# Moving the base inverse's steps and the state update's work between VectorE, ScalarE and PSUM in a delta-rule attention kernel

## The chip, the cores and the metric

The kernel runs on 1 core of a Trainium2 chip, as one program. The metric is the time of an execution in device microseconds. PE is TensorE (PEld its weight loads), DVE is VectorE, ACT is ScalarE, POOL is GpSimd, and SP is SyncE, which issues most DMAs.

## The reference

The input x is [2, 1024, 512] in float32. Four blocks are added to it in turn: a gated delta-rule attention (A), a feed-forward block with 4-bit weights, a state-space scan, and the feed-forward block again. The change touches only A. Cut to what matters, A computes, for each batch and each of 32 value heads (two share one key head; keys and values have 128 channels):

```python
q, k, v = split(silu(causal_conv4(x @ w_qkv)))      # 16, 16 and 32 heads of 128
beta, g = sigmoid(x @ w_b), -exp(A_log) * softplus(x @ w_a + dt_bias)
q, k = l2norm(q) / sqrt(128), l2norm(k)
def step(state, q_t, k_t, v_t, g_t, b_t):           # for each of the 1024 tokens
    state = state * exp(g_t)
    delta = (v_t - k_t @ state) * b_t
    state = state + outer(k_t, delta)
    return state, q_t @ state
core = norm_w * rmsnorm(outs) * silu(x @ w_z)
x = x + core @ w_out
```

## The kernel before

**Units and slots.** The work of the attention is cut into 32 units: a unit is one batch and one key head with its two value heads (REP = 2). The 1024 tokens are 8 chunks of 128 (NC = 8). Every engine runs a loop over slots, 8 slots per unit, and in each slot does pieces of several units at different stages: `unit_at_only(slot, offset)` gives the unit n with slot = 8 n + offset. The order of instructions in each engine's queue is written out by hand, and engines wait for each other by semaphores (`wait_ge`, `then_inc`). In the text, **place k** is a slot whose number modulo 8 is k. A unit starts its projections at offset 0, the convolution's taps at offsets 2, 4, 6 and 8, its decay weights at 8 to 11, the Gram products at 8 to 13, the inverse at 10 to 19, the scan over its chunks at offset 16 + t (t = 0 to 7, so chunk t of some unit is at place t), and the output product at 23 + t.

**The scan of one chunk, t > 0, in a slot.** PE multiplies K with the state (L712, into bank KB), then Q with the state (L717) and transposes K (L719), both into QB. DVE makes the residual from K's product (L1333). PE runs product "a" and perhaps "b" of a later unit's projection (L676), turns a finished o (L761), and multiplies the triangular inverse with the residual (L780), into bank UB. ACT copies that to `u` (L1046). After product "c", PE multiplies the scaled K with u (L810, the addition to the state, into KB) and the decay-weighted Q K product with u (L814, into UB). ACT scales Q's product by exp(gc) into `q_state` (L958) and K by a weight into `k_scaled` (L967). DVE updates the state from KB (L1406; a copy L1399 for t = 0) and adds `q_state` to UB's product into `o` (L1417; a copy L1414 for t = 0). ACT squares o for the norm (L1127). Then PE does the output product (L831), which needs DVE's gated `oT` (L1291), made from L761.

**The base inverse.** Each unit has two halves (a = 0, 1) of four chunks. The inverse of the 16 x 16 blocks is done on DVE by `base_inverse`: section 0 (L1167 to L1178) turns and masks the blocks, and then 14 steps j = 1 to 14, each a shuffle (L1186), a product (L1188) and a sum (L1190) whose width is 8 j; last the identity is added (L1194). Before the change, half 0 does section 0 at offset 10 behind the gate and half 1 at the end of offset 14; steps 1 to 6 (section 1) come at offset 11 + 4a behind the taps, steps 7 to 10 (section 2) at the end of that slot, steps 11 to 14 with the identity (section 3) at the end of offset 12 + 4a. POOL masks the result into `inv` (L1519), DVE turns it (L1198) and PE widens it to 128 x 128 in three levels (L605 to L627), for which ACT makes negated copies `off` (L1068, L1074, L1075, L1081, L1082) and copies back (L1108 to L1116). L608 waits for L1068, and L617 for the last L1075.

**Other work on the path.** The projection's products are read out by ACT (`read_product`, L910 to L917) and, two of seven, by DVE (L1277). ACT starts the convolution with the last tap (L1008), waiting for the reads of both; DVE adds three taps (L1306): two in the middle of the slot, one after the o addition. ACT's SiLU is at places 5 and 1 with two table loads around it. `decay` gets a subtraction on DVE (L1371), a select on POOL (L1505) and an exponential on ACT (L1092), for half 0 at offset 8 and for half 1 at offsets 9, 9 and 11. L910 to L917, L1008 and the u copy L1046 stand in one queue: ACT takes them in the order in which the slot lists them.

Of the kernel before, what the change touches and what calls it, by code (L numbers as in the profile page):

```python
# [13 lines left out]
P = 128  # L14
# [179 lines left out]
def unit_at_only(slot, offset):  # L194
# [10 lines left out]
    rows_turned xn_turned gate_sum gc_sum gc_turned product sums ss_turned g_pair v_turned inv_pe ks qs_kt u_pe s_pe a_pe  # L205
    oT_pe wout_pe
    taps rate ln_a xnT softplus_a e_gc gc_rows act_read tap3 silu ss_copy ln norm_exp chunk_exp decay_exp v_evict q_state
    k_scaled u_copy squares z_silu rstd_ln rstd inv_act
    stats xn gate_in softplus g_in gc gates dve_read conv col_beta decay_sub lT a_weight base inv_dve resid state o_add
# [5 lines left out]
def attention(nc, ctx, c, banks, dram, x_in, x_out, early):  # L215
    on = signals(nc, ctx, ATTENTION_SIGNALS)
    with ExitStack() as st:
# [38 lines left out]
        state, resid, u, q_state = (sb(name, [P, REP, P]) for name in ("state", "resid", "u", "q_state"))  # L256
# [258 lines left out]
        def tensor(e):  # L515
# [184 lines left out]
            for slot in range(ATTENTION_SLOTS):  # L700
# [63 lines left out]
                if n_scan is not None:  # L764
# [11 lines left out]
                    if at > 0:  # L776
                        e.wait_ge(on["o_add"], at)
                    for r in range(REP):
                        rhs = resid[:, r, :] if t > 0 else v_tok[:, N % 2, 0, r, :]
                        made = e.matmul(two(UB, 0)[:, r, :], invT[:, t, r, :], rhs, start=True, stop=True)  # L780
# [19 lines left out]
                if n_scan is not None:  # L800
# [5 lines left out]
                    if t % HALF == 0:  # L806
                        e.wait_ge(on["a_weight"], 4 * N + 2 * (t // HALF) + 2)
                    if t < NC - 1:
                        for r in range(REP):
                            made = e.matmul(two(KB, REP * P)[:, r, :], k_scaled[:, r, :], u[:, r, :],  # L810
                                            start=True, stop=True)
                        made.then_inc(on["s_pe"], 1)
                    for r in range(REP):
                        made = e.matmul(two(UB, REP * P)[:, r, :], decay[:, s, r, t, :], u[:, r, :],  # L814
                                        start=True, stop=True)
# [33 lines left out]
        def scalar(e):  # L849
# [92 lines left out]
            for slot in range(ATTENTION_SLOTS):  # L942
# [8 lines left out]
                if n_scan is not None:  # L951
# [3 lines left out]
                    if t > 0:  # L955
                        e.wait_ge(on["o_add"], at)
                        for r in range(REP):
                            made = e.activation(q_state[:, r, :], two(QB, 0)[:, r, :], ACT.Copy,  # L958
                                                scale=e_gc[:, N // HK, REP * (N % HK) + r, t:t + 1])
                        made.then_inc(on["q_state"], 1)  # L960
# [4 lines left out]
                    if t < NC - 1:  # L965
# [3 lines left out]
                        made.then_inc(on["k_scaled"], 1)  # L969

# [9 lines left out]
                for a in range(2):  # L980
                    n = unit_at_only(slot, 5 + 4 * a)
                    if n is not None:
                        N = n
                        e.wait_ge(on[f"decay{a}{N % 2}"], 16 * (N // 2 + 1))
                        if n >= 2:
                            e.wait_ge(on["state"], LINKS * (N - 2) + 4 * a + 4 - a)
# [1467 lines left out]
```

## Time and profile before

| | us |
|---|---|
| median of 3 runs (lowest to highest) | 4167.84 (4165.18 to 4172.16) |
| the profiled execution | 4168.05 |
| its span, first to last instruction | 4166.1 |
| PE busy | 3997.3 (96%) |
| DVE busy | 3196.9 (77%) |
| ACT busy | 2592.6 (62%) |
| POOL busy | 958.8 (23%) |

The attention takes about the first 3000 us of the span; the mean granted clock of TensorE was 0.991 of its full speed. Busy time is a share of the whole span, so an engine at 77% can still be full for whole slots. In the timeline a row has start, duration, engine, line, operation, out<-in, shapes and count; "[0.45 <-DVE resid L1333]" says that the engine stood idle for 0.45 us before it and what ended that. Consecutive instructions of one line are merged, and the next instruction of a queue may start shortly before the last one's end. The rows of one unit are shown, from about 1800 to 1888 us.

### The profile page before, as it was taken

What the parts mean: (1) busy time and instruction counts of PE and PEld (TensorE: products, weight loads), DVE (VectorE), ACT (ScalarE), POOL (GpSimd) and SP (SyncE); (2) the same over time, 40 slices, a digit from 0 to 9 for tenths busy, and PEclk for the clock granted to TensorE, in tenths of its full rate; (3) what the DMA queues carried; (4) which work ended last, traced back from release to release, by engine and by line L of the source; (5) the groups of instructions that cost most, each with busy time, mean ns of one, the idle gap of its engine ahead of it and who ended that gap; (6) DMA issues with size and microseconds to landing.
All of it is one profiled execution on the core that took longest, in us unless ns stands there. A gap on an engine that the chain in (4) does not pass through costs nothing. (4 is left out here: it accounts for less than half of the span.)

```text
span 4166.1 us, 83038 instructions
## 1 busy us (share of the span) xinstructions
PE 3997.3 (96%) x29437; PEld 2282.0 (55%) x29437; DVE 3196.9 (77%) x8334; ACT 2592.6 (62%) x6087; POOL 958.8 (23%) x1110
## 2 busy tenths in 40 slices
PE   7999999999999999999999999998899999999999
PEld 4555556556555555566565555555444444444444
DVE  4777887787787777877778877777447989898940
ACT  3566676666666666666666666666445656574643
POOL 1224333234333243333333333332100000000000
PEclk9999999999999999999999999999999999999999
DMA  3223334333433433343334333334304545454510
GB/s 131 83 72 84 87 86 90 85 80 85 92 77 85 120 82 85 90 86 85 81 87 92 75 87 85 82 80 97 83 1 132 164 148 168 147 175 153 183 57 10
DMA packets 290733, 402.99 MB, mean 97 GB/s; under 512 B 25774, under 2 KB 125362, under 8 KB 290258
## 3 DMA queue, kind: packets, MB, share of 16 engines
q1 hardware_dynamic: 253458, 330.57, 26.1%
q0 software_dynamic: 36864, 67.13, 12.0%
q8 instruction: 236, 3.87, 0.4%
q14 instruction: 175, 1.43, 0.1%
HBM read 288.56 MB, written 113.25 MB: 96 GB/s over the span
## 5 line engine op out<-in xcount | busy, mean ns | idle before, releaser
L676 PE MATMUL bank<-x_blocks,rows_b 128*128 128x512 f32 x1536 | 713.0, 597 | 0.9 <-ACT partial L914 0.9
L1306 DVE SCALAR_TENSOR_TENSOR conv<-raw,conv_w,conv 128x1024 f32<-128x1024 f32 x384 | 522.7, 1361 | 61.9 <-ACT conv L1008 56.8
L676 PE MATMUL bank<-x_blocks,w_pair 128*128 128x512 f32 x1152 | 549.9, 605 | 14.8 <-DVE x_blocks L1277 4.5
L831 PE MATMUL bank<-w_out_unit,oT 128*128 128x512 f32 x1008 | 491.4, 610 | 0.9 <-ACT out_stage L931 0.9
L676 PEld LDWEIGHTS bank<-x_blocks,rows_b 128*128 128x128 f32 x1536 | 274.9, 190 | 249.1 <-issue 231.3
L1662 PE MATMUL bank<-xnT_f,w_gu 128*128 128x512 f32 x704 | 324.5, 605 | 1.2 <-ACT xnT_f L2161 0.9
L1291 DVE SCALAR_TENSOR_TENSOR oT<-bank,norm_w,z 128x256 f32<-128x256 f32 x252 | 119.2, 473 | 261.4 <-PE bank L761 260.3
L676 PEld LDWEIGHTS bank<-x_blocks,w_pair 128*128 128x128 f32 x1152 | 206.8, 193 | 205.5 <-issue 169.5
L2231 ACT ACTIVATE step_decay<-dt,rate 128x512 f32<-128x512 f32 x256 | 183.4, 720 | 217.1 <-DVE h L2340 215.0
L1681 PE MATMUL bank<-w_down,hidden 128*128 128x512 f32 x704 | 316.9, 594 | 1.7 <-DVE x_blocks L1740 1.7
L1671 PE MATMUL bank<-xnT_f,w_gu 128*128 128x512 f32 x704 | 316.8, 593 | 0.5 <-DVE hidden L1702 0.5
L1127 ACT ACTIVATE k_scaled<-o 128x128 f32<-128x128 f32 x512 | 154.0, 302 | 227.5 <-DVE o L1417 175.4
L1469 POOL DMA_DIRECT2D x_after<-out_stage x256 | 223.0, 904 | 149.8 <-ACT out_stage L931 144.6
L831 PEld LDWEIGHTS bank<-w_out_unit,oT 128*128 128x128 f32 x1008 | 173.1, 192 | 128.0 <-issue 121.9
L1519 POOL TENSOR_TENSOR inv<-n_base,slot_mask 128x512 f32<-128x512 f32 x64 | 81.5, 1274 | 647.7 <-DVE n_base L1194 647.7
L1188 DVE TENSOR_TENSOR rows_b<-rows_b 128x8 f32<-128x8 f32 (+13 forms) x896 | 200.2, 223 | 30.8
L1190 DVE TENSOR_TENSOR n_base<-n_base,rows_b 128x8 f32<-128x8 f32 (+13 forms) x896 | 199.7, 223 | 30.8
L931 ACT COPY out_stage<-bank 128x512 f32<-128x512 f32 x256 | 148.4, 580 | 108.4 <-PE bank L831 99.9
L1681 PEld LDWEIGHTS bank<-w_down,hidden 128*128 128x128 f32 x704 | 130.4, 191 | 152.0 <-issue 151.9
L1662 PEld LDWEIGHTS bank<-xnT_f,w_gu 128*128 128x128 f32 x704 | 132.7, 195 | 147.2 <-issue 145.7
L1671 PEld LDWEIGHTS bank<-xnT_f,w_gu 128*128 128x128 f32 x704 | 130.8, 191 | 149.9 <-issue 148.2
L1186 DVE STREAM_SHUFFLE rows_b<-n_base 128x8 f32<-128x8 f32 (+13 forms) x896 | 207.2, 231 | 0.0
(270 smaller groups left out, 8360.8 us busy)
## 6 DMA issues: line engine op xcount, KB each, us to landing
x_after<-out_stage POOLq DMA_DIRECT2D x256, 256.0 KB, 4.2
rows_b<-bc_rows SPq DMA_DIRECT2D x256, 256.0 KB, 3.6
rows_c<-bc_rows SPq DMA_DIRECT2D x256, 256.0 KB, 3.7
w_pair<-in_w_qkv SPq DMA_DIRECT2D x128, 256.0 KB, 3.9
decay<-gc_rows SPq DMA_DIRECT2D x64, 512.0 KB, 5.0
z<-z_rows SPq DMA_DIRECT2D x64, 512.0 KB, 5.1
z_rows<-x_blocks SPq DMA_DIRECT2D x96, 256.0 KB, 5.8
w_pair<-in_w_z SPq DMA_DIRECT2D x64, 256.0 KB, 3.3
```

Source lines behind the costliest of these rows:

```text
L676: made = e.matmul(bank[:, :], weight[:, j, :], part(0, m)[:, j, :], start=j == 0 and m in (1, 5), stop=j == 1, skip_group_check=True)
L831: made = e.matmul(out_rows(N, t)[:, :], turned_to(N, t)[:, r, :], w_out[:, N % 2, r, :], start=r == 0, stop=r == REP - 1)
L1127: made = e.activation(squares[:, r, :], o[:, at % O_RING, r, :], ACT.Square, accum_out=o_rstd[:, N % 2, t, r:r + 1])
L1186: e.stream_shuffle(row, cols, lanes).then_inc(on["base"], 1)
L1188: e.tensor_tensor(row, row, col, ALU.mult).then_inc(on["base"], 1)
L1190: e.tensor_tensor(cols, cols, row, ALU.add).then_inc(on["base"], 1)
L1306: e.scalar_tensor_tensor(acc, raw[:, i, tap:tap + T], conv_w[:, tap, col:col + 1], acc, ALU.mult, ALU.add).then_inc(on["conv"], 1)
L1469: e.dma_start(x_out[n // HK][t * P:(t + 1) * P, :], out_stage[:, at % STAGES, :], accum_op=ALU.add).then_inc(on[f"x_added{at % STAGES}"], 16)
L1662: made = e.matmul(GB[:, :], w_gu[:, j, i * P:(i + 1) * P], xnT[:, R % 2, j, :], start=j == 0, stop=j == KT - 1)
L1671: made = e.matmul(UB[:, :], w_gu[:, j, INNER + i * P:INNER + (i + 1) * P], xnT[:, R % 2, j, :], start=j == 0, stop=j == KT - 1)
L1681: made = e.matmul(DB[t][:, :], hidden[:, U % 2, t * P:(t + 1) * P], w_down[:, i, :], start=i == 0, stop=i == IT - 1)
L2231: e.activation(step_decay[:, (p + 2) % DECAY_RING, :], dt[:, (KT * q + i) % 2, :], ACT.Exp, scale=rate[:, i, n:n + 1]).then_inc(on["step_d ...
```

## The change

Three things are changed. (1) The base inverse has five sections in place of four, with other slots and earlier points in them: section 0 at offset 10 + 4a, steps 1 to 3 at 11 + 4a and steps 11 to 14 at 12 + 4a all stand ahead of the "a" read and the gate; steps 4 to 10 stand behind the middle taps and ahead of the "b" read. The subtraction and the select for half 1 go from offset 9 to 10. (2) The state's sum and o's sum are formed in PSUM: ACT writes Q's scaled product and (t = 1 to 6) the scaled old state into bank UB, and L810 and L814 add to them there (start=False). DVE then only copies the state out, once both are done. (3) ACT copies o out of UB in place of DVE's addition. The product of L780 goes to bank KB. In front of its seeds ACT now makes `k_scaled`.

```diff
             e.wait_ge(on["inv_dve"], INV_STEPS * (2 * N + t // HALF + 1))
-        if at > 0:
-            e.wait_ge(on["o_add"], at)
         for r in range(REP):
             rhs = resid[:, r, :] if t > 0 else v_tok[:, N % 2, 0, r, :]
-            made = e.matmul(two(UB, 0)[:, r, :], invT[:, t, r, :], rhs, start=True, stop=True)
+            made = e.matmul(two(KB, REP * P)[:, r, :], invT[:, t, r, :], rhs, start=True, stop=True)
         made.then_inc(on["u_pe"], 1)
...
             e.wait_ge(on["a_weight"], 4 * N + 2 * (t // HALF) + 2)
+        if t > 0:
+            e.wait_ge(on["seeded"], LINKS * N + t)
+        elif at > 0:
+            e.wait_ge(on["o_copy"], at)
         if t < NC - 1:
             for r in range(REP):
-                made = e.matmul(two(KB, REP * P)[:, r, :], k_scaled[:, r, :], u[:, r, :],
-                                start=True, stop=True)
-            made.then_inc(on["s_pe"], 1)
+                made = e.matmul(two(UB, 0)[:, r, :], k_scaled[:, r, :], u[:, r, :],
+                                start=t == 0 and r == 0, stop=True, skip_group_check=True)
         for r in range(REP):
             made = e.matmul(two(UB, REP * P)[:, r, :], decay[:, s, r, t, :], u[:, r, :],
-                            start=True, stop=True)
+                            start=False, stop=True, skip_group_check=True)
         made.then_inc(on["a_pe"], 1)
...
         e.wait_ge(on["qs_kt"], at + 1)
-        if t > 0:
-            e.wait_ge(on["o_add"], at)
-            for r in range(REP):
-                made = e.activation(q_state[:, r, :], two(QB, 0)[:, r, :], ACT.Copy,
-                                    scale=e_gc[:, N // HK, REP * (N % HK) + r, t:t + 1])
-            made.then_inc(on["q_state"], 1)
         if t % HALF == 0:
...
             made.then_inc(on["k_scaled"], 1)
+        if t > 0:
+            e.wait_ge(on["o_copy"], at)
+            for r in range(REP):
+                made = e.activation(two(UB, REP * P)[:, r, :], two(QB, 0)[:, r, :], ACT.Copy,
+                                    scale=e_gc[:, N // HK, REP * (N % HK) + r, t:t + 1])
+            if 0 < t < NC - 1:
+                e.wait_ge(on["state"], LINKS * N + t)
+                e.wait_ge(on["chunk_exp"], 2 * N + t // HALF + 1)
+                for r in range(REP):
+                    made = e.activation(two(UB, 0)[:, r, :], state[:, r, :], ACT.Copy,
+                                        scale=chunk_decay[:, N % 2, r, t:t + 1])
+            made.then_inc(on["seeded"], 1)
...
             if n >= 2:
-                e.wait_ge(on["state"], LINKS * (N - 2) + 4 * a + 4 - a)
+                e.wait_ge(on["seeded"], LINKS * (N - 2) + 4 * a + 4 - a)
             e.activation(chunk_decay[:, N % 2, :, HALF * a:HALF * (a + 1)],
...
         e.wait_ge(on["u_pe"], 8 * (n_scan) + t_scan + 1)
-        e.mul(u[:, :, :], two(UB, 0), 1.0 if t_scan == 0 else -1.0).then_inc(on["u_copy"], 1)
+        e.mul(u[:, :, :], two(KB, REP * P), 1.0 if t_scan == 0 else -1.0).then_inc(on["u_copy"], 1)
...
         at = 8 * N + t
-        e.wait_ge(on["o_add"], at + 1)
+        e.wait_ge(on["a_pe"], at + 1)
+        if t < NC - 1:
+            e.wait_ge(on["state"], LINKS * N + t + 1)
+        if at >= O_RING:
+            e.wait_ge(on["oT_pe"], at - O_RING + 1)
+        e.copy(o[:, at % O_RING, :, :], two(UB, REP * P)).then_inc(on["o_copy"], 1)
+        e.wait_ge(on["o_copy"], at + 1)
         if at > 0:
...
     for j in range(1, BASE - 1):
-        if section == (1 if j < 7 else 2 if j < 11 else 3):
+        if section == (1 if j < 4 else 2 if j < 7 else 3 if j < 11 else 4):
             lanes = [16 * (lane // 16) + j for lane in range(32)]
...
         done += 3
-    if section == 3:
+    if section == 4:
         e.wait_ge(on["base"], done)
...
     for a in range(2):
-        n = unit_at_only(slot, 8 + a)
+        n = unit_at_only(slot, 8 + 2 * a)
         if n is not None:
...
             turn_base()
+    for a in range(2):
+        for section, at in ((0, 10), (1, 11), (4, 12)):
+            n = unit_at_only(slot, at + 4 * a)
+            if n is not None:
+                base_inverse(n, a, section)
     read_at(slot, "a")
     gate_out(slot)
-    n = unit_at_only(slot, 10)
-    if n is not None:
-        base_inverse(n, 0, 0)
     convolve(slot, (2, 1))
         if n is not None:
-            base_inverse(n, a, 1)
+            base_inverse(n, a, 2)
+            base_inverse(n, a, 3)
...
         at = 8 * N + t
-        if t == 0:
-            e.wait_ge(on["s_pe"], LINKS * N + 1)
-            e.tensor_copy(state[:, :, :], two(KB, REP * P)).then_inc(on["state"], 1)
-        elif t < NC - 1:
-            e.wait_ge(on["s_pe"], LINKS * N + t + 1)
-            if t in (1, HALF):
-                e.wait_ge(on["chunk_exp"], 2 * N + t // HALF + 1)
-            e.wait_ge(on["state"], LINKS * N + t)
-            for r in range(REP):
-                made = e.scalar_tensor_tensor(
-                    state[:, r, :], state[:, r, :], chunk_decay[:, N % 2, r, t:t + 1],
-                    two(KB, REP * P)[:, r, :], ALU.mult, ALU.add)
-            made.then_inc(on["state"], 1)
-        e.wait_ge(on["a_pe"], at + 1)
-        if at >= O_RING:
-            e.wait_ge(on["oT_pe"], at - O_RING + 1)
-        if t == 0:
-            e.tensor_copy(o[:, at % O_RING, :, :], two(UB, REP * P)).then_inc(on["o_add"], 1)
-        else:
-            e.wait_ge(on["q_state"], LINKS * N + t)
-            e.tensor_tensor(o[:, at % O_RING, :, :], two(UB, REP * P), q_state[:, :, :], ALU.add).then_inc(
-                on["o_add"], 1)
+        if t < NC - 1:
+            e.wait_ge(on["a_pe"], at + 1)
+            e.tensor_copy(state[:, :, :], two(UB, 0)).then_inc(on["state"], 1)
...
             turn_inverse(a)
-        n = unit_at_only(slot, 10 + 4 * a)
-        if n is not None and a == 1:
-            base_inverse(n, a, 0)
-        n = unit_at_only(slot, 11 + 4 * a)
-        if n is not None:
-            base_inverse(n, a, 2)
-        n = unit_at_only(slot, 12 + 4 * a)
-        if n is not None:
-            base_inverse(n, a, 3)
+
         def gpsimd(e):
...
     for a in range(2):
-        n = unit_at_only(slot, 8 + a)
+        n = unit_at_only(slot, 8 + 2 * a)
         if n is not None:
             e.wait_ge(on["decay_sub"], 2 * N + a + 1)
```

## Rows read from the trace of the kernel before

**Rows 1.** The page, part 1: busy time of each engine.

```profile
PE 3997.3 (96%) x29437; PEld 2282.0 (55%) x29437; DVE 3196.9 (77%) x8334; ACT 2592.6 (62%) x6087; POOL 958.8 (23%) x1110
```

**Rows 2.** The waits of PE: engine line, waited for, us, times, longest.

```profile
PE bank L780 <- DVE resid L1333: 52.5, 64, 4.2
```

**Rows 3.** Timeline of PE, places 5 and 1: start, us, what, idle before.

```profile
1815.54 0.71 PE L780 MATMUL bank<-resid,invT 128*128 128x128 f32 x4 [0.45 <-DVE resid L1333]
...
1858.60 0.71 PE L780 MATMUL bank<-resid,invT 128*128 128x128 f32 x4 [1.02 <-DVE resid L1333]
```

**Rows 4.** Groups by line, whole span: busy us, mean ns, idle before.

```profile
L1406 DVE SCALAR_TENSOR_TENSOR state<-state,chunk_decay,bank 128x128 f32<-128x128 f32 x384 | 115.6, 343 | 46.6 <-PE bank L810 38.6 <-issue 0.2
...
L1417 DVE TENSOR_TENSOR o<-bank,q_state 128x256 f32<-128x256 f32 x224 | 93.4, 417 | 2.0 <-PE bank L814 2.0
...
L1371 DVE TENSOR_TENSOR decay<-decay,col_beta 128x1024 f32<-128x1024 f32 x64 | 78.1, 1220 | 3.7 <-DVE col_beta L1365 0.5
...
L958 ACT ACTIVATE q_state<-bank,e_gc 128x128 f32<-128x128 f32 x448 | 140.0, 365 | 79.1 <-PE bank L719 57.7 <-PE bank L717 21.4
```

**Rows 5.** Timeline of DVE, place 7 to place 1.

```profile
1838.62 0.48 DVE L1291 SCALAR_TENSOR_TENSOR oT<-bank,norm_w,z 128x256 f32<-128x256 f32 x1 [1.24 <-PE bank L761]
...
1840.98 0.18 DVE L1186 STREAM_SHUFFLE rows_b<-n_base 128x32 f32<-128x32 f32 x1
...
1848.94 3.36 DVE L1306 SCALAR_TENSOR_TENSOR conv<-raw,conv_w,conv 128x1024 f32<-128x1024 f32 x2
...
1852.22 0.41 DVE L1399 COPY state<-bank 128x256 f32<-128x256 f32 x1
...
1854.09 0.25 DVE L1186 STREAM_SHUFFLE rows_b<-n_base 128x88 f32<-128x88 f32 x1
...
1857.94 0.60 DVE L1333 SCALAR_TENSOR_TENSOR resid<-bank,e_gc,v_tok 128x128 f32<-128x128 f32 x2
```

**Rows 6.** Timeline of POOL, place 0.

```profile
1848.78 1.09 POOL L1505 TENSOR_SCALAR_AFFINE_SELECT decay<-decay 128x1024 f32<-128x1024 f32 x1 [2.78 <-DVE decay L1371]
```

**Rows 7.** Timeline of PE, place 1.

```profile
1852.69 0.70 PE L712 MATMUL bank<-state,kq 128*128 128x256 f32 x2
...
1863.80 0.75 PE L608 MATMUL bank<-off,inv_turned 32*32 32x32 f32 x64
```

**Rows 8.** Timeline of ACT, place 1.

```profile
1853.00 0.31 ACT L1127 ACTIVATE k_scaled<-o 128x128 f32<-128x128 f32 x1 [1.61 <-DVE o L1414]
...
1855.68 0.58 ACT L914 COPY partial<-bank 128x512 f32<-128x512 f32 x1 [0.48 <-PE bank L676]
...
1862.71 0.47 ACT L1068 ACTIVATE off<-bank,neg_odd 128x256 f32<-128x256 f32 x1
```

**Rows 9.** Timeline of DVE, place 2.

```profile
1866.94 0.61 DVE L1333 SCALAR_TENSOR_TENSOR resid<-bank,e_gc,v_tok 128x128 f32<-128x128 f32 x2
...
1869.20 0.69 DVE L1277 TENSOR_TENSOR raw<-bank,partial 128x512 f32<-128x512 f32 x1 [1.65 <-PE bank L676]
...
1871.54 1.83 DVE L1167 STREAM_TRANSPOSE l_quads<-lT 32x256 f32<-32x256 f32 x4
...
1874.46 2.60 DVE L1306 SCALAR_TENSOR_TENSOR conv<-raw,conv_w,conv 128x1024 f32<-128x1024 f32 x2
```

**Rows 10.** Timeline of ACT, and of PE in the last row, place 2.

```profile
1869.92 1.15 ACT L1008 ACTIVATE conv<-raw,conv_w 128x1024 f32<-128x1024 f32 x1 [1.31 <-DVE raw L1277]
...
1874.02 0.27 ACT L1075 ACTIVATE off<-bank 32x128 f32<-32x128 f32 x1
...
1875.10 0.22 PE L617 MATMUL bank<-invT,off 32*32 32x32 f32 x2
```

**Rows 11.** Timeline of ACT, and of PE in the last row, place 5.

```profile
1813.19 0.58 ACT L917 COPY raw<-bank 128x512 f32<-128x512 f32 x1 [0.58 <-PE bank L676]
...
1820.26 0.47 ACT L1068 ACTIVATE off<-bank,neg_odd 128x256 f32<-128x256 f32 x1
...
1820.87 0.74 PE L608 MATMUL bank<-off,inv_turned 32*32 32x32 f32 x64
```

More of the change, by code:

```diff
@@ L204 @@
     z_store0 z_store1 z_store2 z_load0 z_load1
-    rows_turned xn_turned gate_sum gc_sum gc_turned product sums ss_turned g_pair v_turned inv_pe ks qs_kt u_pe s_pe a_pe
+    rows_turned xn_turned gate_sum gc_sum gc_turned product sums ss_turned g_pair v_turned inv_pe ks qs_kt u_pe a_pe
     oT_pe wout_pe
-    taps rate ln_a xnT softplus_a e_gc gc_rows act_read tap3 silu ss_copy ln norm_exp chunk_exp decay_exp v_evict q_state
+    taps rate ln_a xnT softplus_a e_gc gc_rows act_read tap3 silu ss_copy ln norm_exp chunk_exp decay_exp v_evict seeded o_copy
     k_scaled u_copy squares z_silu rstd_ln rstd inv_act
-    stats xn gate_in softplus g_in gc gates dve_read conv col_beta decay_sub lT a_weight base inv_dve resid state o_add
+    stats xn gate_in softplus g_in gc gates dve_read conv col_beta decay_sub lT a_weight base inv_dve resid state
     part_sum oT_copy out_copy
@@ L255, in attention @@
         oT = sb("oT", [P, REP, P])
-        state, resid, u, q_state = (sb(name, [P, REP, P]) for name in ("state", "resid", "u", "q_state"))
+        state, resid, u = (sb(name, [P, REP, P]) for name in ("state", "resid", "u"))
         k_scaled = sb("k_scaled", [P, REP, P])
```

## The prediction, made before the change was run

> **What bounds the kernel now.** I read the page first. PE is busy for 3997 of 4166 us [rows 1], so nothing that leaves PE's own work alone can win more than the 169 us in which it idles. The change leaves it alone: every matmul stays, with the same shapes. So the question is what PE waits for. The waits of PE have one entry that stands out: L780, the product of the inverse with the residual, waits 52.5 us in 64 pieces for L1333, the residual that DVE makes [rows 2]. 64 is two per unit, and the timeline shows them: 0.45 us at place 5 and 1.02 us at place 1 [rows 3]. A place is the slot number modulo 8, so each comes once per unit. All 32 units look alike (32 x 1.47 = 47 us), so one unit worked out at its places gives the whole.
>
> DVE is late there because of the base inverse: at the end of places 4 and 0 it runs the last steps, widths 88 to 112, and only then the residual. At place 0 that is from 1854.09 to 1857.94, and the residual comes right behind [rows 5]. The change takes this chain out of the residual's way. Whether it wins depends on what those steps are put in front of instead.
>
> **Work that moves between engines.** DVE loses L1406 (115.6 us) and L1417 (93.4 us) [rows 4] and gets a copy of 0.41 us per slot [rows 5], 192 of them (places 1 to 6) beyond the 32 that it makes now: 209 - 79, or 130 us less in all, about 4 us per unit. ACT gets the o copy (256 slots; I take 0.37 us from L958's mean) and a second pair of scaled copies at places 1 to 6, at 0.6 us a pair (L958: 140.0 us for 224 pairs [rows 4]): 95 + 115 = 210 us. ACT is at 2593 us [rows 1], so it has room on the average. These totals cost PE nothing by themselves; what counts is where each engine has no idle time before something that PE needs. The new wait of L810 for the seeds costs nothing: ACT queues them before the u copy, which L810 waits for anyway. What it may cost is 0.6 us on the u copy; cover is PE's own product c, which runs between L780 and L810. The copy to state now waits for the second pair of matmuls (L814) too, some 0.5 us, covered by the output product that PE runs before it needs the state. The decay subtraction of half 1 goes from place 1 to place 2. No DMA is moved; SP keeps its waits. On POOL the mask comes earlier and the select of half 1 one slot later, both with slack.
>
> **Place 0 to 1: the state is late.** From the gate at 1838.62 (place 7, started by PE) DVE has no idle time until the state copy at 1852.22 [rows 5]: 13.60 us of queue. PE starts the next slot at 1852.69, 0.06 us after that copy ends [rows 7]. So the margin is nil, and what is added to this stretch is paid. What goes: the first three steps of the inverse (1839.03 to 1840.98, 1.95 us), which now run before the gate in idle time, and an o addition (0.42, [rows 4]). What comes: the last four steps with the identity (1854.09 to 1857.94, 3.85 us), now ahead of gate, taps and state. 13.60 - 1.95 - 0.42 + 3.85 = 15.08: the state is 1.48 us later, and PE with it. The stall of 1.02 us at L780 is then gone (only one tap, half of 2.60 us [rows 9], is queued between the state and the residual), which leaves 0.46.
>
> The same slot's end on ACT: its squares started at 1853.00, behind the o of DVE [rows 8]. Now the state copy ends at 1854.11, the o copy takes 0.37 and the squares start near 1854.55, 1.55 later. ACT then has one idle piece of 0.48 us before L914 [rows 8], against 0.6 us of new seeds: 1.55 + 0.12 = 1.67 us late when it comes, behind two table loads and the silus, to L1068, which starts now at 1862.71 and takes 0.47. That gives 1864.85, and PE takes 0.14 us to follow it (1820.73 to 1820.87 [rows 11]): L608 at 1864.99 where it was 1863.80 [rows 7]. **Cost: 1.2 us**, in 31 units (the last has no next unit beside it).
>
> **Place 2: the first tap is late.** Here the base inverse's section 0 and the moved subtraction are put ahead of the product read L1277. Section 0 takes 1871.54 to 1874.46, 2.92 us [rows 9], the subtraction 1.22 [rows 4]. DVE idles 1.65 us before that read now [rows 9], so the read is 4.14 - 1.65 = 2.5 us later. ACT's tap L1008 waits for exactly this read [rows 10] and stands before the u copy and the copies L1074 and L1075 in its queue. The last of these ends at 1874.29 now and PE wants it at 1875.10 [rows 10]. Later by 2.5 it ends at 1876.8, and L617 starts at 1876.9, 1.8 us late. ACT has small waits in between that shrink; I take **1.5 us**, in the 30 units in which section 0 and the tap fall together. Bounds: 0, if the work were hidden, and 2.5.
>
> **Place 5: the win is given back.** L780's 0.45 us goes here, since place 4 has room: the steps go where DVE now waits for the gate's transpose. But L608 follows ACT's L1068 by only 0.14 us (1820.26 + 0.47 against 1820.87 [rows 11]): ACT sets that moment, from a product read at 1813.19 which itself waits for PE and has 0.58 us of idle before it [rows 11], about the seeds' 0.6. So ACT is no earlier and PE waits there instead. Gain 0, bounds 0 and 0.45.
>
> **Sum**, against the profiled execution's own 4168.05 us: 31 x 1.2 + 30 x 1.5 = 37 + 45 = 82 us, so 4250. The median of the runs is 4167.84, the same.
>
> **Two prices not seen in the trace.** (a) No ACT copy from SBUF into PSUM. Nearest is L958, from PSUM: 0.6 us a pair; between 0.4 and 0.75 a place-1 chain moves by 0.2. (b) DVE beside POOL. The two taps at place 0 take 3.36 us with POOL's select beside them and 2.60 at place 2 [rows 5, 6, 9]: 0.76 us lost. The 3.28 us to the state copy in my sum hold that loss once. After the change the select falls beside the moved steps, and POOL's mask, which follows the moved steps, can fall beside the taps. Between no loss (the state 0.76 earlier) and a second one (0.76 later) I keep one.
>
> **Rivals.**
> A, faster, 0.16: the spread works as written. For it: the 52.5 us [rows 2] are real and DVE has 130 us less to do. If every stall at L780 goes and nothing takes its place, 4168 - 52 = 4116. With ACT setting L608 at places 1 and 5, the win is the slack at place 1 only (L608 at 1863.80, ACT ready at 1862.71 + 0.47 + 0.14 = 1863.32: 0.48 us): 4168 - 15 = 4153. It decides at the state copy of place 0: if DVE reaches it no later than 0.5 us after now, no loss. Against: the margin of 0.06 [rows 5, 7].
> B, only place 0 costs, 0.18: the read at place 2 is late but ACT catches up before L617. 4168 + 37 = 4205.
> C, POOL's mask beside DVE, 0.12: what the select did to the taps [rows 5, 6] happens twice at place 0. 31 x 0.76 = 24 more: 4274. The Trainium skill, SBUF — State Buffer (Who interferes with whom), has a rule: a DVE operation with two SBUF inputs and a GpSimd operation that reads SBUF exclude each other for the whole instruction. By that rule, the trace agrees for the select beside the taps, if not for its full 1.09 us [rows 6]; and by it a mask over the taps would cost as C says.
> D, ACT becomes the bound, 0.08: 0.6 us of seeds reach PE at all of the 192 slots: 4168 + 115 = 4283. Against: at place 4 and 6 ACT idles beside product reads now.
> E, even, 0.06: the losses equal the 15 to 30 us won.
> The forecast, both places costing as worked out, 0.40; its own range is 4215 to 4285.
>
> **Numbers.** Faster: A, 0.16; within 0.2% (8 us, about what the measurement can tell from no change): E, 0.06; slower: the rest, 0.78. The range runs from 4140 (the upper part of A) to 4285 (C, the bounds of place 2), leaving out the clean win and the worst of C and D.
>
> **What would show it.** L780's wait for L1333 near 0 in every case. If I am right: PE's L712 waits for the state L1399's successor about 1.5 us once per unit; L617 waits for L1075 about 1.5 us once per unit; L608 waits for L1068 by 0.7 us at place 1 and 0.5 at place 5; ACT's L1008 waits for L1277 near 4 us at place 2; the unit is 2.5 us longer. If L617 does not wait, the step at place 2 is wrong; if L712 does not, the one at place 0; if PE's waits in the scan are all below 0.1 us, A holds. PE's busy time should stay at 3997 us: if it grows, the accumulating matmuls cost more than the plain ones, which I excluded.

## The result, and the profile after the change

The changed kernel takes **4362.99 us** (median of 5 runs, 4356.47 to 4363.45), where the kernel before took 4165.18 us beside it (4162.54 to 4172.16): a ratio of **1.0466**, 95% interval 1.0450 to 1.0481. It is 198 us slower. The forecast was 82 us slower, 4250, with a range up to 4285: the sign was right, the size was not.

First the page of the changed kernel, its span and part 1, against [rows 1]:

```profile
span 4360.9 us, 83006 instructions
...
PE 4026.4 (92%) x29437; PEld 2284.0 (52%) x29437; DVE 3238.2 (74%) x7886; ACT 2771.1 (64%) x6727; POOL 1029.3 (24%) x1110
```

PE issues the same 29437 matmuls. DVE is busy 41 us longer, though it lost the sums for the state and o. The first two experiments (e1, e2) separate this: with the PSUM part alone DVE is busy 3083.9 us, 113 less than before (the forecast had 130), and with the spread alone 3354.4 us, 157.5 more, with the same 8334 instructions as before. So with the spread the same instructions take longer; the rows below show some of them beside POOL. ACT and POOL are busy longer too. Next the waits of PE (engine, what line waited for what, us in total, times, longest). The one entry of [rows 2], L780's wait for the residual, is no longer among the large ones. In its place stand nine others ("..." stands for a single wait at the start):

```profile
PE bank L608 <- ACT off L1075: 43.7, 62, 1.7
PE bank L676 <- DVE raw L1290: 43.7, 33, 2.6
PE bank L617 <- ACT off L1082: 34.2, 31, 1.1
PE bank L832 <- DVE oT L1304: 30.0, 32, 1.3
PE bank L712 <- DVE state L1415: 27.4, 31, 1.6
PE bank L574 <- ACT v_tok L877: 19.6, 31, 2.1
PE bank L676 <- ACT bank L911: 17.8, 35, 1.5
PE bank L812 <- ACT u L1053: 16.5, 14, 2.6
...
PE bank L676 <- DVE z_extra L1290: 13.4, 29, 0.5
```

Eight of the nine come once per unit (29 to 35 times, L608 twice). Adding them up by place over the steady part, PE now waits 7.04 us per unit where it waited 1.99; the unit, measured from one col_beta of DVE to the next (the small addition with which DVE starts a unit's decay weights), went from 88.24 to 93.97 us. From the first col_beta to the 32nd the changed kernel takes 174 us longer; 21 more lie behind the last one, in the drain of the attention. That is the 195 us between the two profiled spans.

**Place 0 to 1**, the timeline of PE in one unit, then of DVE and POOL (start, us, what, idle before in brackets). They answer to [rows 3, 7], [rows 5] and [rows 6]. The kernel after has other line numbers: L676 is still the projection's product, L832 the output product (L831), L812 and L815 the products with u (L810, L814), L1290 the product read (L1277), L1304 the gate (L1291), L1319 the taps (L1306), L1199 to L1203 the steps of the base inverse (L1186 to L1190), L1415 the state copy:

```profile
1394.03 1.98 PE L676 MATMUL bank<-x_blocks,w_pair 128*128 128x512 f32 x4 [0.46 <-DVE z_extra L1290]
...
1400.58 1.98 PE L832 MATMUL bank<-w_out_unit,oT 128*128 128x512 f32 x4 [0.93 <-DVE oT L1304]
...
1404.31 0.70 PE L712 MATMUL bank<-state,kq 128*128 128x256 f32 x2 [0.88 <-DVE state L1415]
...
1415.07 0.74 PE L608 MATMUL bank<-off,inv_turned 32*32 32x32 f32 x64 [1.07 <-ACT off L1075]
```

```profile
1393.30 0.68 DVE L1290 TENSOR_TENSOR z_extra<-bank,partial 128x512 f32<-128x512 f32 x1
...
1395.31 0.26 DVE L1199 STREAM_SHUFFLE rows_b<-n_base 128x88 f32<-128x88 f32 x1
...
1400.05 0.48 DVE L1304 SCALAR_TENSOR_TENSOR oT<-bank,norm_w,z 128x256 f32<-128x256 f32 x1
...
1400.44 3.48 DVE L1319 SCALAR_TENSOR_TENSOR conv<-raw,conv_w,conv 128x1024 f32<-128x1024 f32 x2
...
1403.84 0.41 DVE L1415 COPY state<-bank 128x256 f32<-128x256 f32 x1
...
1404.18 2.86 DVE L1319 SCALAR_TENSOR_TENSOR conv<-raw,conv_w,conv 128x1024 f32<-128x1024 f32 x1
```

```profile
1395.54 1.10 POOL L1494 TENSOR_SCALAR_AFFINE_SELECT decay<-decay 128x1024 f32<-128x1024 f32 x1
...
1400.56 2.28 POOL L1508 TENSOR_TENSOR inv<-n_base,slot_mask 128x512 f32<-128x512 f32 x1
...
1404.06 1.90 POOL L1487 TENSOR_TENSOR o<-o,o_rstd 128x1024 f32<-128x1024 f32 x1
```

The forecast had two waits here: some 1.5 us at L712 for the state, and 0.7 at L608. The rows have four. PE waits 0.46 us for the read L1290, 0.93 for the gate L1304, 0.88 for the state L1415, then 1.07 for ACT's copy at L608. The read is the last one of place 7: it starts at 1393.30, ahead of the steps of place 0. What stands in front of it are steps 4 to 10 of half 1 (the last ends at 1393.37), which the change put ahead of the "b" read; before, steps 7 to 10 came behind it. The forecast had nothing for place 7. The moved steps run from 1395.31 to the gate at 1400.05, 4.74 us where they took 3.85 in [rows 5], with POOL's select (1395.54 to 1396.64) beside them. Then POOL's mask runs beside the two taps: 2.28 us for the mask, 3.48 for the taps. And POOL's next big operation, the scaling of o (L1487, 1404.06 to 1405.96), now falls on the third tap, which takes 2.86 us; a single tap is half of 2.60 us [rows 9]. PE does not pay for that tap: L778, the product behind the residual (L780 before), does not wait in these slots.

**Place 2**, DVE, then ACT and PE, against [rows 9, 10]:

```profile
1419.85 1.83 DVE L1180 STREAM_TRANSPOSE l_quads<-lT 32x256 f32<-32x256 f32 x4
...
1421.72 1.20 DVE L1183 TENSOR_TENSOR rows_b<-l_quads,strict_even 128x128 f32<-128x128 f32 x1
...
1423.15 0.70 DVE L1189 TENSOR_TENSOR n_base<-rows_b 128x128 f32<-128x128 f32 x1
...
1424.10 0.68 DVE L1290 TENSOR_TENSOR raw<-bank,partial 128x512 f32<-128x512 f32 x1
```

```profile
1424.81 1.15 ACT L1015 ACTIVATE conv<-raw,conv_w 128x1024 f32<-128x1024 f32 x1 [4.38 <-DVE raw L1290]
...
1428.62 0.27 ACT L1082 ACTIVATE off<-bank 32x128 f32<-32x128 f32 x1
...
1424.83 1.98 PE L676 MATMUL bank<-x_blocks,w_pair 128*128 128x512 f32 x4 [1.21 <-DVE raw L1290]
...
1429.04 0.22 PE L617 MATMUL bank<-invT,off 32*32 32x32 f32 x2 [1.10 <-ACT off L1082]
```

Section 0 takes from 1419.85 to 1424.10, 4.25 us, not 2.92. Two of its TENSOR_TENSORs take 1.20 us (L1183) and 0.70 us (L1189), and both are 0.30 on the average before the change. The read L1290 comes behind it, and two engines hang on that read: ACT's tap waits 4.38 us for it, as forecast, and PE's own next product L676 waits 1.21, which was not in the forecast. L617's wait of 1.10 comes on top, where 1.5 was forecast.

### The profile page after: what moved, and what is told of

Same layout as the page of the kernel before. It is cut to its first block and busy times, and to the rows that moved or that the text cites. A ratio compares the mean times of both kernels' runs of the same rounds, so it can differ in the third digit from the quotient of the medians.

```text
span 4360.9 us, 83006 instructions
## 1 busy us (share of the span) xinstructions
PE 4026.4 (92%) x29437; PEld 2284.0 (52%) x29437; DVE 3238.2 (74%) x7886; ACT 2771.1 (64%) x6727; POOL 1029.3 (24%) x1110
## 3 DMA queue, kind: packets, MB, share of 16 engines
q14 instruction: 176, 1.44, 0.1%
## 5 line engine op out<-in xcount | busy, mean ns | idle before, releaser
L676 PE MATMUL bank<-x_blocks,rows_b 128*128 128x512 f32 x1536 | 717.1, 600 | 0.9 <-ACT partial L915 0.9
L1319 DVE SCALAR_TENSOR_TENSOR conv<-raw,conv_w,conv 128x1024 f32<-128x1024 f32 x384 | 597.8, 1557 | 70.5 <-ACT conv L1015 65.3
L676 PE MATMUL bank<-x_blocks,w_pair 128*128 128x512 f32 x1152 | 557.1, 611 | 82.4 <-DVE raw L1290 43.7
L832 PE MATMUL bank<-w_out_unit,oT 128*128 128x512 f32 x1008 | 502.1, 621 | 31.0 <-DVE oT L1304 30.0
L676 PEld LDWEIGHTS bank<-x_blocks,rows_b 128*128 128x128 f32 x1536 | 274.4, 190 | 252.7 <-issue 232.0
L676 PEld LDWEIGHTS bank<-x_blocks,w_pair 128*128 128x128 f32 x1152 | 202.1, 191 | 291.9 <-issue 170.3
L1346 DVE SCALAR_TENSOR_TENSOR resid<-bank,e_gc,v_tok 128x128 f32<-128x128 f32 x448 | 135.6, 343 | 241.3 <-PE bank L712 241.3
L832 PEld LDWEIGHTS bank<-w_out_unit,oT 128*128 128x128 f32 x1008 | 175.0, 194 | 167.3 <-issue 125.3
L1201 DVE TENSOR_TENSOR rows_b<-rows_b 128x8 f32<-128x8 f32 (+13 forms) x896 | 227.1, 253 | 30.9
L1015 ACT ACTIVATE conv<-raw,conv_w 128x1024 f32<-128x1024 f32 x128 | 149.4, 1167 | 142.5 <-DVE raw L1290 142.5
L1133 ACT COPY o<-bank 128x256 f32<-128x256 f32 x256 | 95.1, 372 | 226.2 <-DVE state L1415 220.5
L1449 POOL TENSOR_TENSOR rows_b<-w_pair 128x256 f32<-128x256 f32 x192 | 166.2, 866 | 306.0 <-PE bank L676 300.4
L1203 DVE TENSOR_TENSOR n_base<-n_base,rows_b 128x8 f32<-128x8 f32 (+13 forms) x896 | 213.6, 238 | 30.8
L932 ACT COPY out_stage<-bank 128x512 f32<-128x512 f32 x256 | 145.8, 570 | 116.3 <-PE bank L832 113.1
```

The costliest lines, as they stand in the source:

```text
L676: made = e.matmul(bank[:, :], weight[:, j, :], part(0, m)[:, j, :], start=j == 0 and m in (1, 5), stop=j == 1, skip_group_check=True)
L832: made = e.matmul(out_rows(N, t)[:, :], turned_to(N, t)[:, r, :], w_out[:, N % 2, r, :], start=r == 0, stop=r == REP - 1)
L1015: e.activation(conv[:, p % 3, :], raw[:, i, PAD:PAD + T], ACT.Copy, scale=conv_w[:, PAD, col:col + 1]).then_inc(on["tap3"], 1)
L1201: e.tensor_tensor(row, row, col, ALU.mult).then_inc(on["base"], 1)
L1203: e.tensor_tensor(cols, cols, row, ALU.add).then_inc(on["base"], 1)
L1319: e.scalar_tensor_tensor(acc, raw[:, i, tap:tap + T], conv_w[:, tap, col:col + 1], acc, ALU.mult, ALU.add).then_inc(on["conv"], 1)
```

## Experiments

**The two parts apart.** The first kernel is the old one with the new order of the base inverse and the later subtraction; the second is the changed one with the old order, so that only the PSUM part is left.

```diff
 e1_spread_only (from before)
-  if section == (1 if j < 7 else 2 if j < 11 else 3):
+  if section == (1 if j < 4 else 2 if j < 7 else 3 if j < 11 else 4):
-  n = unit_at_only(slot, 8 + a)
+  n = unit_at_only(slot, 8 + 2 * a)
+  for section, at in ((0, 10), (1, 11), (4, 12)):   # ahead of reads and gate
+      n = unit_at_only(slot, at + 4 * a)
+      base_inverse(n, a, section)
```

> The kernel before with the base inverse spread as in the change (and the half-1 subtraction and select one slot later), state and o still summed by DVE. Theory 1, the order of DVE's queue is the loss: the state at place 0 and the read at place 2 come as late as in the changed kernel or 0.4 us later, so about 4360 to 4420 us, 195 to 250 above before. Theory 2, the work given to ACT is the loss: without it the spread wins its stalls, 4115 to 4160 us.

Measured: 4338.50 us, ratio 1.0412 (1.0396 to 1.0427), 172 us slower, 22 below the expected range. Theory 1 holds in kind.

> The change with the base inverse, the subtraction and the select put back where they were before: only the seeds in PSUM, the sums there and ACT's o copy are left. Theory 1: DVE has 130 us less and ACT only idle time to lose; the stall at L780's successor shrinks from 1.02 and 0.45 us to about 0.3 and 0, ACT's copy before L608 keeps part of it: 4140 to 4165 us. Theory 2: most of the 198 us stay, 4300 us or more.

Measured: 4201.42 us, 1.0082 (1.0067 to 1.0097), 35 us slower. That is a miss: the PSUM part is no gain, but a loss of its own. 172 and 35 make 207 against 198, so the two nearly add up. The waits of PE in this second kernel:

```profile
PE bank L778 <- DVE resid L1346: 28.6, 38, 2.8
PE bank L761 <- ACT out_stage L932: 19.8, 33, 2.2
PE bank L574 <- ACT v_tok L877: 19.4, 31, 2.1
PE bank L608 <- ACT off L1075: 16.2, 31, 1.7
```

Three of them are waits for ACT's copies (L877, L932, L1075), which were 2.0, 5.2 and 2.3 us before. The fourth is the residual's: its stall at place 1 is gone, and that at place 5 is 0.71 us instead of 0.45. This points at where ACT's new work stands in its queue. The unit takes 88.91 us instead of 88.24, some 20 of the 35 us; some 12 more lie in the drain. The forecast's term "These totals cost PE nothing by themselves" is not borne out.

**The two places apart.** Each kernel is the changed one with one section of the base inverse put back behind what it had been put ahead of; e5 does both.

```diff
 e3_place2_back
-  if n is not None:
+  if n is not None and (section, a) != (0, 0):
...
+  n = unit_at_only(slot, 10)          # behind the gate, as before
+  if n is not None:
+      base_inverse(n, 0, 0)
```

> The changed kernel with section 0 of half 0 (place 2) back behind the read and the gate; all else as changed. Theory 1: the waits of PE that hang on the late read at place 2 (the product behind it 1.22 us, L617 1.10, L574 0.55 per unit) go, 2.9 us x 30 = 86 us, so about 4277 us. Theory 2: the order is not what counts, under 20 us change.

Measured: 4281.64 us, 1.0277 (1.0262 to 1.0293): 81 us less than the changed kernel. The waits at L676 for the read and at L617 are gone. The wait of L574 for v_tok, which the expectation counted too, stays at 0.55 us per unit; it is in the PSUM part alone as well.

```diff
 e4_place0_back
-  if n is not None:
+  if n is not None and (section, a) != (4, 1):
...
+  n = unit_at_only(slot, 12 + 4 * a)  # at the slot's end, as before
+  if n is not None and a == 1:
+      base_inverse(n, a, 4)
```

> The changed kernel with the last steps of half 1 (place 0) back at the end of the slot; all else as changed. Theory 1: PE's waits for the gate (0.95 us), for the state (0.85) and 1.0 of the 1.07 us for ACT's copy before L608 go, against a returned stall at the residual of 0.5 to 1.0 us: about 2.1 us x 31 = 65 us less, 4290 to 4310 us. Theory 2: under 20 us change.

Measured: 4282.64 us, 1.0274 (1.0257 to 1.0291): 80 us less, 7 below the expected range. The waits for the gate and the state are gone, L608's at place 1 has only shrunk from 1.07 to 0.95 us, and the stall at the residual, expected back with 0.5 to 1.0 us, did not return. The wait of 0.46 us for the read of place 7 is still there.

> The changed kernel with both pieces back: section 0 of half 0 behind the read and the gate, the last steps of half 1 at the end of place 0. Theory 1 (two separate late places in DVE's queue, plus a third cost that is ACT's): the two gains of 81 and 80 us add up, 4190 to 4210 us, and what is left over before, about 35 us, is what the PSUM part alone costs. Theory 2 (one lateness that the two places share): the second undoing gains little, 4240 us or more.

Measured: 4201.54 us, 1.0084 (1.0068 to 1.0099): 161.5 us less, the sum of 81.4 and 80.4, and the same time as with the PSUM part alone. So these two placements hold the spread's whole net loss, and each costs 80 us, 2.6 us per unit. The rest of the spread only exchanges waits: without the residual's stall PE now waits 0.47 us for the read of place 7, 0.46 at L676 for ACT's read L911 and 1.20 at L608 per unit, and the time is the same.

**POOL beside DVE.** The mask of half 1 additionally waits for the state copy of place 0, so that it no longer runs beside the first two taps.

```diff
 e6_mask_late (from the changed kernel, POOL)
+  if a == 1:
+      e.wait_ge(on["state"], LINKS * n + 1)
```

> The changed kernel in which POOL's mask of half 1 (place 0) also waits for DVE's state copy of that slot, so that it no longer runs beside the taps; the values are the same. Theory 1 (DVE's taps with two SBUF inputs stand still while POOL reads SBUF): the two taps fall from 3.48 to about 2.6 us, the state copy and ACT behind it come 0.9 us sooner, 31 x 0.85 = 27 us less, 4330 to 4345 us. Theory 2 (the taps are long for another reason): 4355 to 4370 us.

Measured: 4334.75 us, 1.0400 (1.0382 to 1.0417): 28 us less for one wait more on POOL. PE's wait for the state at L712, 0.88 us per unit, is gone; the one for the gate (0.94) and the one at L608 (1.07) are as they were. The groups of the taps by line (busy us, mean ns of one), first in the changed kernel, then in this one:

```profile
L1319 DVE SCALAR_TENSOR_TENSOR conv<-raw,conv_w,conv 128x1024 f32<-128x1024 f32 x384 | 597.8, 1557 | 70.5 <-ACT conv L1015 65.3
```

```profile
L1319 DVE SCALAR_TENSOR_TENSOR conv<-raw,conv_w,conv 128x1024 f32<-128x1024 f32 x384 | 523.3, 1363 | 71.7 <-ACT conv L1015 66.5
```

Then the timeline of this kernel at place 0, DVE and POOL:

```profile
1388.55 2.60 DVE L1319 SCALAR_TENSOR_TENSOR conv<-raw,conv_w,conv 128x1024 f32<-128x1024 f32 x2
...
1391.39 1.28 DVE L1319 SCALAR_TENSOR_TENSOR conv<-raw,conv_w,conv 128x1024 f32<-128x1024 f32 x1
```

```profile
1391.66 2.15 POOL L1510 TENSOR_TENSOR inv<-n_base,slot_mask 128x512 f32<-128x512 f32 x1 [2.97 <-DVE state L1415]
```

The pair is back at 2.60 us, the third tap at 1.28, and the mean at 1363 ns. The mask, now beside the third tap, still takes 2.15 us, but the tap, which had begun first, keeps its 1.28. This is rival C's mechanism, at nearly its price (24 us).

**ACT's queue.** Next, the PSUM part alone with its seeds moved from the head of ACT's slot to just ahead of the u copy.

```diff
 e7_seeds_late (from e2_psum_only, ACT)
-  if t > 0:                            # behind k_scaled, early in the slot
-      e.wait_ge(on["o_copy"], at)
-      ...
-      made.then_inc(on["seeded"], 1)
...
+  if t > 0:                            # right ahead of the u copy
+      e.wait_ge(on["o_copy"], at)
+      ...
+      made.then_inc(on["seeded"], 1)
```

> The PSUM part alone (order of the base inverse as before) with ACT's two pairs of seeds moved from behind the K copy to right before the u copy, where ACT mostly waits for PE. Theory 1 (the 35 us are ACT's order: seeds ahead of the v copies at place 3, ahead of the tap at places 4 and 0): PE's wait for the v copy of 0.54 us goes and the stall at the residual at place 5 shrinks from 0.71 to 0.3: 4160 to 4180 us. Theory 2 (it is ACT's amount of work): 4195 to 4210 us.

Measured: 4245.86 us, 1.0184 (1.0169 to 1.0199), 44 us more than e2_psum_only, where 20 to 40 less were expected. The waits of PE say why:

```profile
PE bank L608 <- ACT off L1077: 89.3, 62, 1.7
```

The waits for v_tok and the residual are gone, as expected. L608 has grown from 16.2 to 89.3 us, at both places 1 and 5: there ACT runs its silus without a pause up to the copy that sets L608, and two seed pairs (0.60 and 0.68 us) ahead of it are paid in full: 2.93 us per unit at the two places, where it was 0.43. So one position isn't right for all slots. The next kernel seeds early at t = 1 and 5 and late elsewhere.

```diff
 e11_seeds_mixed (from e2_psum_only, ACT)
-  if t > 0:
+  if t % HALF == 1:
...
+  if t > 0 and t % HALF != 1:          # right ahead of the u copy
```

> The PSUM part alone, with the seeds right before the u copy except at places 1 and 5 (the silu slots), where they stay behind the K copy. Theory 1 (late seeds are right where ACT waits for PE afterwards, wrong where it runs without a pause up to the copy for L608, which cost 1.6 and 1.2 us per unit with all seeds late): 4246 less 32 x 2.3 = 74 us, 4165 to 4180 us. Theory 2 (the seeds cost the same wherever they stand): 4200 us or more.

Measured: 4168.28 us, 1.0013 (1.0004 to 1.0022), 5 us above the kernel before measured beside it (4163.19). So about 30 of the 35 us were the seeds' position.

**A spread that fits.** The old kernel, with only those steps moved that fall in DVE's idle time: section 0 of half 0 stays behind the gate, steps 7 to 14 of half 1 stay at the ends of their slots (so the read of place 7 keeps its place too), and so does the subtraction.

```diff
 e8_spread_fit (from before, DVE)
+  for section, at in ((0, 10), (1, 11), (4, 12)):
+      n = unit_at_only(slot, at + 4 * a)
+      if n is not None and (section, a) not in ((0, 0), (4, 1)):
+          base_inverse(n, a, section)
...
+  base_inverse(n, a, 2)
+  if a == 0:
+      base_inverse(n, a, 3)            # half 1: sections 3 and 4 at the slots' ends
```

> The kernel before (state and o summed by DVE) with the change's spread of the base inverse, less what was late: section 0 of half 0 stays behind the gate, half 1 keeps steps 7 to 14 at the ends of its slots, the half-1 subtraction stays where it was. Theory 1: PE's stalls at the residual (1.02 and 0.45 us per unit) go; at place 5 ACT's reads behind the silus take the win back, at place 1 ACT's copy before the second inverse product leaves 0.5 to 0.9 us: 4135 to 4155 us. Theory 2 (any spread costs): above 4165 us.

Measured: 4161.95 us, 0.9987 (0.9978 to 0.9996). That is 6 us less than the kernel before beside it (4168.36), and 7 above the expected range. The residual's stalls, 1.47 us per unit before [rows 3], are gone, and the time has hardly moved. Its waits of PE:

```profile
PE bank L608 <- ACT off L1068: 29.2, 61, 1.7
PE bank L676 <- ACT bank L910: 17.8, 35, 1.4
```

L608 waits for ACT at place 1 (0.63 us) and place 5 (0.26), and L676 for ACT's product read L910 (0.46). That is 1.35 us of the 1.47 back. So ACT's order was changed: the second product read goes ahead of the silus in slots that load their table, and the copy for L608 ahead of the z silu.

```diff
 e9_fit_act_order (from e8_spread_fit, ACT)
+  if slot > 8:
+      read_at(slot, "b")               # ahead of the silus
...
-  read_at(slot, "b")
+  if slot <= 8 or (n_qk is None and n_v is None and n_z is None):
+      read_at(slot, "b")
...
+  e.wait_ge(on["inv_pe"], 6 * H + 1)   # ahead of the z silu
+  e.activation(off[:, :, 0:32], tile_ps, ACT.Copy, scale=c["neg_odd"][:, 0:1]).then_inc(on["inv_act"], 1)
```

> The fitted spread (state and o summed by DVE) with two moves in ACT's queue: in slots with a table load the read of product b stands ahead of the silus, and ACT's copy for the second inverse product (L1068) ahead of z's silu and its table load. Theory 1 (the residual's stall went, and ACT's late read and copy at places 5 and 1 took it back: 0.46, 0.26 and 0.63 us per unit): 32 x 1.35 = 43 us below the 4162 of the fitted spread, 4112 to 4130 us. Theory 2 (PE simply has no more to give): 4155 us or more.

Measured: **4103.39 us, 0.9856 (0.9842 to 0.9871)**: 60 us below the kernel before measured beside it, some 255 to 260 below the changed one, and 9 below the expected range. None of the three waits is left. The control is the same ACT order on the old kernel:

> The kernel before with the same two moves in ACT's queue and nothing else. Theory 1 (the two bounds are in series: without the spread DVE's residual is what PE waits for): nearly nothing, 4158 to 4168 us. Theory 2 (ACT's order alone is worth the gain): below 4140 us.

Measured: 4157.28 us, 0.9987 (0.9977 to 0.9997), 1 below the range of theory 1. The residual's stalls are all there (53.2 us at L780). Each edit alone gives 0.13%, both together 1.44%: the two waits stood one behind the other, and taking away one only uncovers the other. The window from 1000 to 1600 us shows how much PE still idles (PE, PEld, DVE, ACT and POOL busy, granted clock, DMA share, GB/s), before and then with both edits:

```profile
1000.00:1600.00 600.00, 585.93 (x5492) 356.75 (x5489) 479.65 (x1439) 408.21 (x1068) 205.50 (x234) 1.00 0.40 91
```

```profile
1000.00:1600.00 600.00, 597.92 (x5639) 365.40 (x5638) 496.55 (x1463) 416.39 (x1101) 225.97 (x238) 1.00 0.40 93
```

PE goes from 585.93 to 597.92 of 600 us. It is now bound by its own work in the steady part: the page of this kernel has PE at 97%.

```profile
PE 3986.6 (97%) x29437; PEld 2276.5 (55%) x29437; DVE 3223.4 (79%) x8334; ACT 2584.9 (63%) x6087; POOL 1047.4 (26%) x1110
```

> The changed kernel with the fitted spread, the mixed seeds and ACT's two moves: the PSUM part in the best surroundings found. Theory 1: PE's waits of the scan nearly all go, and only ACT's 210 us more of work may show at the silu slots: 4115 to 4145 us, no better than the same without the PSUM part. Theory 2 (DVE's relief of 130 us is worth something once the order is right): at least 5 us below that kernel.

Measured, with the PSUM part, e11's seeds and both edits: 4109.06 us, 0.9872 (0.9857 to 0.9886), 6 below the expected range. That is no better than without the PSUM part, though DVE is busy 106 us less (3117.3 against 3223.4). The traces say a little more: from the first col_beta to the last the PSUM part is 7 us faster (2643.9 against 2650.9), and behind the last one 13 us slower. Whether the drain could be kept from paying for it was not tried.

## Why the prediction was right or wrong

**The direction and the places: right.** The net loss of the spread is at places 0 and 2, as e3, e4 and e5 show: DVE work was moved from where only the residual waits to where more does. L780's wait went, and didn't pay for it.

**Place 0, forecast 37 us, measured 80: mis-sized.** The step that failed is "the state is 1.48 us later, and PE with it", which became "Cost: 1.2 us". It followed one chain, from the gate of place 7 to the state copy. The moved steps also stand ahead of the gate of place 0, and PE waits there first (0.93 us), then for the state (0.88), and at L608. By the traces of the changed kernel and of e4, PE's waits at this place cost 1.96 us per unit (0.95 gate, 0.88 state, 0.13 at L608) and its busy time grows by 0.53; why it grows was not tested. The sum of the queue was short because of POOL. I kept one loss of 0.76, but the moved steps are stretched by 0.89 (4.74 for 3.85 us) with the select beside them, and the taps by another 0.88 with the mask. e6 takes away the second loss, and with it just the wait for the state: 28 us of the 43 between forecast and measurement. That was rival C. The read of place 7 is a cost of its own, left out of the forecast, and e4 does not bring it back.

The rows look like turns taken for a whole instruction. The third tap starts at 1404.18, L1487 ends at 1405.96, and with 1.28 us of its own from there the tap would end at 1407.24; it ends at 1407.04. The second tap of the pair is this row:

```profile
1401.75 2.17 DVE L1319 SCALAR_TENSOR_TENSOR conv<-raw,conv_w,conv 128x1024 f32<-128x1024 f32 x1
```

The mask ends at 1402.84, so by the same reckoning this tap would end at 1404.12; it ends at 1403.92. The mask's own 2.28 us would be a wait for the first tap. That is the rule of the Trainium skill, SBUF — State Buffer (Who interferes with whom), named with rival C, and the trace agrees but for some 0.2 us each time. e6 shows that the overlap is the cause; that it works by turns is only read from the rows.

**Place 2, forecast 45 us, measured 81: mis-sized.** "ACT's tap L1008 waits for exactly this read" was right, with 4.38 us of wait as forecast, but PE's own next product waits for the same read, and I followed ACT's side alone. The step that failed is the term of 1.5 us for L617: it measured 1.10, and 1.22 at L676 were missing beside it; both are gone in e3, with 0.37 us of PE's busy time. Also section 0 was priced at 2.92 us from a stretch where POOL is still; at its new place it took 4.25.

**Place 5, forecast 0: right in kind.** The win is given back, and a little more: the 0.45 us at L780 became 0.46 at L676 and 0.26 at L608, waits for ACT, so 0.27 us per unit is lost, just outside the bounds of 0 and 0.45 gained. e8, without the PSUM part, has the same two figures; e9 removes them.

**ACT's added work, forecast 0, measured 35: wrong.** I argued from ACT's share and from idle time at places 4 and 6. ACT's queue is in order, and with the early seeds the v copies are late: their wait goes when the seeds move (e7). Moving them all makes L608 late instead. e11 wins back about 30 of the 35. PE's wait of 0.46 us per unit for the copy to `out_stage` (L932) stays in e7, e11 and e12; the o copy stands a few instructions ahead of it in the queue, which makes it the likely cause, but no run moves it. And what follows the last col_beta is 10 to 13 us longer with the PSUM part in each of three pairs (before and e2, e1 and the changed kernel, e9 and e12); the reason stays open. Rival D had ACT as a cost too, but as one in each slot.

**The sum by the runs** is 81 + 80 + 35 = 196, measured 198. Nothing of size is left over. The signs came out in kind and not in size: L712 waits 0.88 us (forecast 1.5), L617 1.10 (1.5), L608 1.07 and 0.26 (0.7 and 0.5), the tap L1015 4.38 (near 4), and the unit is 5.73 us longer, not 2.5.

**PE's busy time** was to stay at 3997 us and is 4026.4. The accumulating matmuls aren't the cause: the spread alone, without them, has 4022.9, and the PSUM part alone, with them, 4000.5. Part of the excess is in the drain. The windows over it, before, after, and with the PSUM part alone:

```profile
2817.00:2955.00 138.00, 115.11 (x1143) 76.11 (x1142) 82.59 (x277) 85.62 (x241) 37.74 (x44) 0.91 0.46 87
```

```profile
2991.00:3150.00 159.00, 123.15 (x1144) 79.55 (x1143) 76.90 (x247) 100.11 (x289) 38.12 (x44) 0.87 0.42 80
```

```profile
2837.00:2988.00 151.00, 120.70 (x1143) 79.50 (x1143) 74.75 (x247) 98.04 (x283) 37.59 (x44) 0.89 0.42 80
```

PE does the same 1143 or 1144 matmuls in 123.15 us instead of 115.11, at a mean granted clock of 0.87 instead of 0.91 (a mix of its levels 1.2 and 2.4 GHz), having idled more there (36 us instead of 23). The PSUM part alone lies between, with 120.70 us at 0.89. The clock isn't all of it: e5 has 117.93 us at 0.91. The other 21 us arise in the steady part, at a granted clock of 1.00: PE is busy 86.25 us per unit before and 86.94 after, 0.69 more, so that a unit's 5.73 us are 5.05 of waits and 0.69 of busy time. With both placements taken back (e5) it is 86.04. So this part belongs to the placements and to the waits that they make; what lengthens the matmuls there is not shown.

## What to carry to other kernels

A wait that ends late is worth its length only if no second chain ends right behind it: here the fitted spread alone and ACT's order alone gave 0.13% each, and both together 1.44%, so look for the second bound before judging the first edit. When work moves ahead in an in-order queue, list everything behind it there that any engine awaits, the reads and the gate as well as the final result, and do so at each place where something moved: place 7 was missed here. Price each moved operation by the row of its own duration beside the neighbour that it will get on POOL, not by its quietest row.

## What was not expected of the hardware

For its length, a small DVE operation suffers more beside POOL than a large one. The 128x128 TENSOR_TENSOR at place 2 took 1.20 us beside POOL's L1449 (1421.74 to 1422.76 in POOL's timeline), four times its 0.30 on the average before, while the pair of taps beside the mask went from 2.60 to 3.48. It looks as if it waited out the neighbour, however short it is itself; no run isolates this. POOL loses too: its 128x512 TENSOR_TENSOR took 1.27 us on the average before, and 2.28 beside the taps. And ACT's copies into PSUM took about as long as those into SBUF: a seed pair at 0.60 us from PSUM to PSUM, 0.62 us for the old pair to SBUF, 0.68 for the pair from SBUF to PSUM.
